# Gram of a DLRM tower: one 32x32 product per sample in two batches, and increments behind each gather instead of a memset

## What is computed

```python
e = jnp.stack([tbl_0[ids[:, 0]], ..., tbl_31[ids[:, 31]]], axis=1)      # 2048 x 32 x 64
gram = jnp.einsum('bnd,bmd->bnm', e, e)                                  # 2048 x 32 x 32
z = gram[:, rows, cols]                                                  # rows, cols = triu_indices(32, k=1)
h = jnp.concatenate([z.reshape(2048, -1), dense_ctx], axis=1)            # 2048 x 512
h = jnp.maximum(h @ W_top1 + b_top1, 0.0)                                # 512
h = jnp.maximum(h @ W_top2 + b_top2, 0.0)                                # 256
y = h @ W_top3                                                           # 1
```

## Time and profile before

| | us |
|---|---|
| median of 3 runs | 505.01 |
| lowest and highest | 502.04, 505.68 |
| the profiled execution | 506.08 |
| its span, from the first to the last instruction | 504.3 |
| busy: PE, POOL, DVE, ACT | 423.6, 417.8, 297.8, 114.6 |

### The profile page before, as it was taken

One profiled execution on the slowest core, in us unless ns is written; L12 is line 12 of the kernel. 1 busy time (PEld: TensorE's weight loads), 2 busy tenths in 40 slices (PEclk: granted clock), 3 DMA queues, 4 the chain that ended last, 5 costly groups with the idle time before them and its releaser, 6 DMA issues.

```text
span 504.3 us, 10183 instructions
## 1 busy us (share of the span) xinstructions
PE 423.6 (84%) x4080; PEld 382.6 (76%) x4080; DVE 297.8 (59%) x361; ACT 114.6 (23%) x206; POOL 417.8 (83%) x538
## 2 busy tenths in 40 slices
PE   5398589995299989979799969988999959993887
PEld 5387479984298879869698869868897949883765
DVE  2599779794094589448483749339753948250400
ACT  2244312131011321123012311132103300230311
POOL 7999999998898899888998989889998899885010
PEclk9699799997599999999799979999899979996999
DMA  4444631012301122112301123112311231111010
GB/s 109 140 141 149 205 137 22 17 33 51 102 15 23 25 60 98 22 26 61 102 17 24 40 57 88 22 27 56 102 21 21 54 84 44 24 35 44 1 43 2
DMA packets 22070, 29.58 MB, mean 59 GB/s; under 512 B 9910, under 2 KB 14198, under 8 KB 20896
## 3 DMA queue, kind: packets, MB, share of 16 engines
q1 hardware_dynamic: 12980, 18.96, 10.9%
q0 software_dynamic: 8640, 8.86, 10.7%
q10 hardware_dynamic: 404, 1.09, 0.5%
HBM read 24.61 MB, written 0.07 MB: 49 GB/s over the span
## 4 chain that ended last, share of the span: by engine, by line
POOL 82%; issue 9%; PE 4%; DMA 2%; SPq 1%; DVE 1%; ACT 1%; DVEq 0%; ACTq 0%
POOL rows L253 59%; POOL pause L260 23%; PE mlp_ps L328 1%; PE gram_ps L316 1%; SPq L192 1%; PE mlp_ps L338 1%; DVE folded L530 1%; ACT folded L441 0%; DMA rows<-tbl,index 0%; PE gram_ps L352 0%; SPq L219 0%; DMA index<-ids 0%; DMA pairs<-dense 0%; DMA pairs<-folded 0%; PE turn_ps L289 0%
## 5 line engine op out<-in xcount | busy, mean ns | idle before, releaser
L253 POOL DMA_INDIRECT rows<-tbl,index x264 | 299.4, 1134 | 45.9 <-issue 43.3
L303 PE MATMUL turn_ps<-split_sb,onehot 125*128 125x192 bf16 x2192 | 210.4, 256 | 19.9 <-DVE split_sb L544 17.3
L303 PEld LDWEIGHTS turn_ps<-split_sb,onehot 125*128 125x128 bf16 x2192 | 192.9, 102 | 27.8 <-DVE split_sb L544 18.7
L495 DVE TENSOR_TENSOR onehot<-place,codes_wide 125x2048 bf16<-125x2048 f16 (+1 forms) x127 | 168.1, 1325 | 7.3 <-DMA place<-ids_scratch 7.3
L260 POOL MEMSET pause<- 128x384 f32 x264 | 115.7, 438 | 0.2
L503 DVE TENSOR_REDUCE rows<-turn_ps 128x128 f32<-128x384 f32 x124 | 68.8, 556 | 70.8 <-PE turn_ps L303 68.1
L530 DVE COPY_PREDICATED folded<-second_sb,gram_ps 128x512 f32<-128x512 int32 x64 | 46.6, 729 | 81.8 <-ACT folded L441 81.7
L316 PE MATMUL gram_ps<-emb_t 64*128 64x128 f32 x1024 | 74.0, 286 | 3.3 <-DVE folded L530 3.3
L316 PEld LDWEIGHTS gram_ps<-emb_t 64*128 64x128 f32 x1024 | 62.7, 190 | 17.7 <-issue 13.3
L289 PE MATMUL mlp_ps<-ident_sb,rows 128*128 128x128 f32 x240 | 39.1, 288 | 40.8 <-DMA rows<-tbl,index 34.5
L441 ACT COPY folded<-gram_ps 128x512 f32<-128x512 f32 x64 | 37.5, 586 | 152.0 <-PE gram_ps L316 152.0
(11 more groups left out here) (28 smaller groups left out, 75.8 us busy)
## 6 DMA issues: line engine op xcount, KB each, us to landing
place<-ids_scratch SPq DMA_DIRECT2D x8, 1000.0 KB
rows<-tbl,index POOLq DMA_INDIRECT x264, 2.7
pairs<-folded SPq DMA_DIRECT2D x122, 32.0 KB
emb_t<-tbl SPq DMA_DIRECT2D x8, 250.0 KB
folded<-tbl SPq DMA_DIRECT2D x5, 312.5 KB
w_sb<-w SPq DMA_DIRECT2D x1, 1024.0 KB
place<-ids_scratch ACTq DMA_DIRECT2D x1, 750.0 KB
rows<-tbl SPq DMA_DIRECT2D x2, 312.5 KB
```

Of the source, the lines that this page charges most:

```text
L253: nc.gpsimd.indirect_dma_start(rows[:, s % 2, slot, t, :], None, tables[f][:, :], bass.IndirectOffsetOnAxis(index[:, s, t, f:f + 1], 0),). ...
L303: last = nc.tensor.matmul(turn_ps[:, u % 2].rearrange("p k b -> p (k b)")[:, t * PARTS * DIM:(t + 1) * PARTS * DIM], onehot[:, u % RING, c ...
L495: nc.vector.tensor_tensor(onehot[:, u % RING, 0:SPAN[u], :], place[:, parity, u, :].unsqueeze(1).to_broadcast([TP, SPAN[u], SUPER]), codes ...
```

## The change

The Gram product is made one sample at a time. `gram_batch` makes 256/2 = 128 products a batch and there are two batches a super tile. A product has the 32 columns of one sample as weights and as moving operand. It stands on the 64 partitions of its half t and writes the 32 partitions of `gram_ps` that belong to i (the sample's place in its quad). The products go i by i, with t innermost. The 32x32 result is all wanted, so a copy and a fold of 128x512 take 128 samples instead of 32: 2 of each a super tile instead of 8.

The step keeps its eight slots (`SLOTS`); the two Gram batches stand in slots 0 and 1 (`GRAM_IN_SLOT`), behind the lookups of these slots. `folded` gets a buffer for each parity and ACT's wait for the moves goes away. The moves start after slot 1. The semaphore `grams_begun` is incremented once a batch on PE.

On POOL the memset and its wait go away, and 12 increments of the semaphore `paused` stand behind each gather. The landing places of some small tables at the start change (`spare`).

```diff
+SLOTS = 8
+GRAM_BATCHES = 2
+GRAM_IN_SLOT = (0, 1)
+BATCH_Q = QUADS // GRAM_BATCHES
...
-PAUSE = 384
+PAUSE = 12
...
-        folded = sb("folded", [P, QUAD, HALF, QUADS], fp32)
+        folded = sb("folded", [P, 2, HALF, QUADS], fp32)
...
-        gram_ps = ps("gram_ps", [P, 2, TILES, BATCH_Q // TILES, 2, QUAD * HALF], fp32)
+        gram_ps = ps("gram_ps", [P, GRAM_BATCHES, TILES, BATCH_Q // TILES, FIELDS], fp32)
...
                         ).then_inc(rows_landed[s % 2][slot // GROUP_F], 16)
-                        before = next(pauses)
-                        if before:
-                            pool.wait_ge(paused, before)
-                        nc.gpsimd.memset(pause[:], 0.0).then_inc(paused, 1)
+                        for _ in range(PAUSE):
+                            pool.sem_inc(paused, 1)
...
             def gram_batch(s, k):
                 pe.wait_ge(second_copied, GRAM_EMPTY + GRAM_BATCHES * s + k - 1)
-                for u in range(BATCH_Q):
-                    quad = BATCH_Q * k + u
-                    t, q = u % TILES, (BATCH_Q * k + u) // TILES
-                    e = emb_t[DIM * t:DIM * (t + 1), QUAD * q:QUAD * (q + 1), :]
-                    last = nc.tensor.matmul(gram_ps[:, k % 2, t, u // TILES].rearrange("p h ij -> p (h ij)"),
-                                            e.rearrange("p b f -> p (b f)"),
-                                            e.rearrange("p b (h j) -> p h b j", h=2),
-                                            start=True, stop=True)
+                pe.sem_inc(grams_begun, 1)
+                for u in range(BATCH_Q // TILES):
+                    for i in range(QUAD):
+                        for t in range(TILES):
+                            e = emb_t[DIM * t:DIM * (t + 1), QUAD * (BATCH_Q // TILES * k + u) + i, :]
+                            last = nc.tensor.matmul(gram_ps[FIELDS * i:FIELDS * (i + 1), k, t, u, :], e, e,
+                                                    start=True, stop=True)
...
-                    gram_batch(s, k)
+                    if k in GRAM_IN_SLOT:
+                        gram_batch(s, GRAM_IN_SLOT.index(k))
...
+            def copy_first(s, k, parity):
+                act.wait_ge(gram_ready, GRAM_BATCHES * s + k + 1)
+                nc.scalar.copy(folded[:, parity, :, BATCH_Q * k:BATCH_Q * (k + 1)].rearrange("p j (q t) -> p j q t", t=TILES),
+                               gram_ps[:, k, :, :, 0:HALF].rearrange("p t q j -> p j q t")).then_inc(first_copied, 1)
...
-                    if k == 0 and (mlp or not ahead):
-                        act.wait_ge(pairs_moved, 16 * len(MOVES) * s)
-                    act.wait_ge(gram_ready, GRAM_BATCHES * s + k + 1)
-                    nc.scalar.copy(folded[:, :, :, BATCH_Q * k:BATCH_Q * (k + 1)].rearrange("p i j (q t) -> p (i j) q t", t=TILES),
-                                   gram_ps[:, k % 2, :, :, 0, :].rearrange("p t q ij -> p ij q t")).then_inc(first_copied, 1)
+                    if k in GRAM_IN_SLOT:
+                        copy_first(s, GRAM_IN_SLOT.index(k), parity)
...
+            def fold_second(s, k, parity):
+
+                dve.wait_ge(first_copied, GRAM_BATCHES * s + k + 1)
+                dve.sem_inc(folds_begun, 1)
+                nc.vector.copy_predicated(
+                    folded[:, parity, :, BATCH_Q * k:BATCH_Q * (k + 1)].rearrange("p j (q t) -> p j q t", t=TILES),
+                    second_sb[:].unsqueeze(2).unsqueeze(2).to_broadcast([P, HALF, BATCH_Q // TILES, TILES]),
+                    gram_ps[:, k, :, :, HALF:FIELDS].rearrange("p t q j -> p j q t")).then_inc(second_copied, 1)
```

More of the change, by code:

```diff
@@ L1 @@
 from contextlib import ExitStack
-from itertools import count
 import numpy as np
@@ L51 @@
 assert [u for units in TURN_UNITS + GRAM_UNITS for u in units] == list(range(UNITS))
-GRAM_UNITS += [[]] * (GRAM_BATCHES - len(GRAM_UNITS))
+GRAM_UNITS += [[]] * (SLOTS - len(GRAM_UNITS))
 READY_MADE = 3
-assert READY_MADE < RING and READY_MADE <= UNITS and not any(GRAM_UNITS[GRAM_BATCHES - READY_MADE + 1:])
+assert READY_MADE < RING and READY_MADE <= UNITS and not any(GRAM_UNITS[SLOTS - READY_MADE + 1:])
 SP_MOVES = 10
-PAUSE = 384
+PAUSE = 12
 MOVES = [(i, jq) for i in range(QUAD) for jq in range(QUAD)]
@@ L87, in slot_meaning @@
     assert sorted(rows.ravel()) == list(range(HIDDEN1))
-    return rows, np.tile(second, (QUAD, QUAD))
+    return rows, np.tile(second, (QUAD, 1))
 def build(nc, ids, tables, dense, w1, b1, w2, b2, w3, identity, second, looked_ids, codes, out):
@@ L114, in build @@
         y = sb("y", [1, BATCH], fp32)
-        pause = sb("pause", [P, PAUSE], fp32)
         w1_sb = sb("w1_sb", [P, CHUNKS, HIDDEN1], fp32)
@@ L121, in build @@
         ident_sb = sb("ident_sb", [P, P], fp32)
-        second_sb = sb("second_sb", [P, QUAD * HALF], i32)
+        second_sb = sb("second_sb", [P, HALF], i32)
         split_sb = sb("split_sb", [TP, SPAN_AT[-1], PARTS, DIM], bf16)
@@ L130, in build @@
         onehot = sb("onehot", [TP, RING, SPAN_MAX, SUPER], bf16)
-        spare = [(8, emb_t[0:TP].rearrange("p b f -> p (b f)")), (6, folded[0:TP].rearrange("p i j q -> p (i j q)")),
-                 (3, rows[0:TP, 1, 0:UNITS].rearrange("p u t d -> p (u t d)"))]
+        spare = [(8, emb_t[0:TP].rearrange("p b f -> p (b f)")), (1, h2[0:TP].rearrange("p o b -> p (o b)")),
+                 (3, folded[0:TP].rearrange("p h j q -> p (h j q)")),
+                 (3, rows[0:TP, 1, 0:UNITS].rearrange("p u t d -> p (u t d)")),
+                 (1, pairs[0:TP, 1].rearrange("p i j q -> p (i j q)"))]
         whole = []
@@ L185, in build @@
         folds_begun = sem("folds_begun")
+        grams_begun = sem("grams_begun")
         block = ctx.enter_context(nc.Block())
@@ L244, in _ @@
         def _(pool):
-            pauses = count()
             def gather(s, begin=UNITS):
@@ L366, in step @@
                     stay_warm(WARM_NEXT)
-                for k in range(GRAM_BATCHES):
+                for k in range(SLOTS):
                     if ahead:
@@ L520, in step @@
                         follow(s + 1, TURN_UNITS[g], 1 - parity)
-                for k in range(GRAM_BATCHES):
+                for k in range(SLOTS):
                     if ahead:
                         follow(s + 1, GRAM_UNITS[k], 1 - parity)
-                        if k >= GRAM_BATCHES - READY_MADE:
-                            make_onehot(s + 2, k - (GRAM_BATCHES - READY_MADE), parity, loads=loads)
+                        if k >= SLOTS - READY_MADE:
+                            make_onehot(s + 2, k - (SLOTS - READY_MADE), parity, loads=loads)
                     if mlp and k == LAYER3_BEFORE:
                         layer3_drain(s - 1)
-                    dve.wait_ge(first_copied, GRAM_BATCHES * s + k + 1)
-                    dve.sem_inc(folds_begun, 1)
-                    nc.vector.copy_predicated(
-                        folded[:, :, :, BATCH_Q * k:BATCH_Q * (k + 1)].rearrange("p i j (q t) -> p (i j) q t", t=TILES),
-                        second_sb[:].unsqueeze(2).unsqueeze(2).to_broadcast([P, QUAD * HALF, BATCH_Q // TILES, TILES]),
-                        gram_ps[:, k % 2, :, :, 1, :].rearrange("p t q ij -> p ij q t")).then_inc(second_copied, 1)
+                    if k in GRAM_IN_SLOT:
+                        fold_second(s, GRAM_IN_SLOT.index(k), parity)
             def take_high(u):
```

6 lines of the change are left out of this document (2 added, 4 removed).

## The result

The changed kernel is much slower: median 694.64 us (678.72 to 705.76, 4 runs) beside 505.35 (502.04 to 505.96, 4 runs), ratio 1.354, 95% interval 1.335 to 1.374. The forecast was 465 us, range 435 to 560. The profiled execution took 700.86 us. Medians and ranges are of all executions; the ratio compares only those that lie within 1.5% of the fastest of their kernel (here 678.72 and 688.42 us).

A forecast was written before the change was run, and what follows sets the result against it. POOL's gathers and memsets were taken to set the pace, with PE the bound once the memsets go: 372.8 + 8 x 11.3 = 463.2 us, with 1.8 around the span and the profiled run 1.1 above the median; predicted 465, range 435 to 560.

The forecast's parts named there:

- It becomes the bound when POOL gets faster: On PE: it has little slack, so its own need sets the time once POOL's 115.7 us of memsets go.
- 372.8 + 8G: Span in us as PE alone would set it: 372.8 without Gram, plus eight super tiles' Gram work.
- G: Gram work of one super tile on PE: 11.3 us taken, 8.7 to 34.8 as bounds.
- signs of being wrong: Gram batch over 8.2 us; 0.4 us gaps before gathers; granted clock falling in Gram batches, or PE standing at their start.
- Record time of a thin product: On PE: 22 ns for each of 512 Gram records a super tile, bounds 17 and 68 ns.
- increments under the gather: On POOL: increments of 0.07 us, 0.84 per gather, run while the gather runs; gather interval 1.3 us.
- increments behind the gather: Rival on POOL: increments run strictly after each gather, interval 2.13 us, POOL stays the bound, 576 us; chance 0.12.
- an unchanged interval: Rival on POOL: gathers come no closer without the memset, span stays near 504 us; chance 0.07.
- the likeliest case: Whole kernel: 17 to 26 ns a Gram record on PE, 444 to 481 us; chance 0.45.
- The pause at the loop's jump: On PE: a stand of 2.4 us, expected to be better covered by the long products of layer 2.
- the tail: From the end of the last Gram product to the end of the span: 28.0 us.
- the fixed price: Rival on PE: thin products do not shrink with their columns; 559 us at 45 ns, 653 at 68; chance 0.17.

The follow-up runs named there:

- e4: Kernel before with nothing behind the gathers, neither memset nor increments: 654.13 us.
- e7: Changed kernel, 12 increments, gathers fetching only 64 of 128 rows from super tile 2 on: 490.32 us.
- e8: Changed kernel without the gathers of super tiles 2 to 7 and their increments: 485.92 us.
- e9: Changed kernel, 12 increments, gathers fetching 128 bytes of each row instead of 256 from super tile 2 on: 484.61 us.
- e16: Changed kernel, 12 increments, gathers fetching 96 of 128 rows from super tile 2 on: 482.42 us.
- e13: Changed kernel with 14 increments behind each gather instead of 12: 486.8 us.
- e12: Kernel before without the gathers and memsets of super tiles 2 to 7: 474.44 us.
- e14: Kernel before with 14 increments behind each gather in place of the memset: 477.87 us.
- e2: Kernel before with 12 increments behind each gather in place of the memset and its wait: 555.96 us.
- e15: Kernel before with 13 increments behind each gather in place of the memset: 468.29 us, ratio 0.927.

## Why the prediction failed, step by step

**"It becomes the bound when POOL gets faster": the step that failed.** The working took PE's need (372.8 + 8G, 51.2 us a step) as independent of what POOL does, and the 115.7 us of memsets as time to be had. In the changed kernel the steps took 80 to 99 us, because while gathers ran PE got two or three products every 0.73 us. In the kernel before, the memset was not just a delay of POOL: with it gone and nothing else changed, the kernel goes from 504 to 654 us (e4, both on chip 8). No rival has PE lose its instructions, so no price and no chance stood for it. One of the signs of being wrong did come, a granted clock that falls in the Gram batches (0.50 from 217 to 238 us). That the memset's absence is not the whole condition, since the same gathers and increments ran without the trickle at the start of e7, e8, e9 and e16, is as far as the runs go; the cause behind it stays open.

**Record time of a thin product.** Forecast 22 ns, bounds 17 to 68. In a stretch undisturbed, e13 has 246 product records within 2.87 us, under 12 ns each on average, below my lower bound. The rule of the Trainium skill ("TensorE: Matmul & The Clock Gate", section "Wait — 56ns, not 53.3ns?") gave 25 ns as a floor; for these records, on alternating row halves, the trace disagrees, and the measurement decides. The timeline of e13:

```profile
238.27 2.87 PE L316 MATMUL gram_ps<-emb_t 64*32 64x32 f32 x246
242.75 0.27 PE L316 MATMUL gram_ps<-emb_t 64*32 64x32 f32 x10 [1.62 <-issue]
242.96 3.47 PE L302 MATMUL turn_ps<-split_sb,onehot 125*128 125x192 bf16 x40
246.36 2.51 PE L316 MATMUL gram_ps<-emb_t 64*32 64x32 f32 x204
250.30 0.65 PE L316 MATMUL gram_ps<-emb_t 64*32 64x32 f32 x52 [1.43 <-issue]
250.88 8.42 PE L302 MATMUL turn_ps<-split_sb,onehot 125*128 125x192 bf16 x100
```

The two batches take 4.69 and 4.52 us up to the next piece, G = 9.2 (forecast 11.3), and a third of it is a pause of 1.6 and 1.4 us in which PE has no instructions. So where G comes out near the forecast it is by luck: the record time was too high, and the pause was not in it. In the changed kernel as it is, the Gram of each of super tiles 1 to 5 took 32 to 39 us: the trickle takes whatever PE has to do while gathers run, lookups too, so no G describes it.

**The thin Gram is worth nothing on PE even then.** Before had 8.7 us a super tile, the thin one 9.2 to 11.8 in e13, pauses included, and after such a pause the next lookups can run at the low clock: in e8, 40 lookup products behind the pause of 2.45 us took 5.1 us at a granted clock of 0.66 instead of 3.4. These two are what the traces show of the 12 us between e12 and e8 (on two chips) and the 9 us between e14 and e13 (on one); their shares were not measured apart.

**POOL: increments under the gather.** Right in kind: 12 increments of 0.0785 us (I took 0.07) are 0.94 us, as long as a gather, and gathers stand 1.25 us apart where POOL catches up; 1.3 was forecast. "Or 12 increments and a start, about 1.0" was wrong: the loop itself needs 0.47 us beside them. The rivals of POOL, increments behind the gather and an unchanged interval, are both refuted.

**The sum for PE alone.** It was too low by itself, by about 30 us, which is more than the half-width of the likeliest case (444 to 481). For the thin Gram with its G of some 10 us it gives 372.8 + 80 + 1.8 = 455; the runs without the trickle have 482 to 490. For the Gram of before it gives 444, and e12 has 474. The steps are part of it: the first Gram product of two successive steps in e13 stands at 238.27 and 286.76, 48.5 us, but the four others between 128 and 395 us are 52 to 58 long, and the five together are 53.4 on average where 39.9 + 10 had been counted. The pause at the loop's jump, which was taken out as a wait, stays (in e13 two of 8.0 us together). Right were the tail (28.4 us from the last Gram product to the end in e13, forecast 28.0) and that the chain moves to PE, with no waits for rows.

**Chances.** "Slower" had 0.25, all of it with the fixed price or with POOL. The kernel ends on that side for neither reason, so that share was right by luck; 694.64 lies above even the bound of 68 ns a record (653).

## What to carry to other kernels

A pause that computes nothing may pay for something that no wait in the profile names: take it out alone before anything is built on its time. Short, regular idle times of an engine with nothing as their releaser mean that its instructions come late; look at what the other queues do in them. Count instructions as a resource: four times as many products with the same columns bought nothing (487 us against 478 with 14 increments, on one chip).

When a run differs from its reference, look first at the part that the edit leaves alone. If that part differs too, as the first two super tiles do here, the edit is not what made the difference. And put the reference itself, not only the kernel before, into every series: the kernel before had 504 to 507 us on each chip and showed nothing of what separates them.

## What the runs showed of the hardware

- While indirect gathers 0.94 us long run at 1.25 to 1.5 us distance, the issue of instructions on PE, and at times on POOL, can be held to one to three in 0.7 us (e4, e2, the changed kernel). The same gathers at the same distance can also run without it (e15, and the start of e8, with 12 increments).
- On one chip, what stood behind the gathers changed the time of the kernel with the Gram of before from 504 us (memset) over 556 (12 increments) to 654 (nothing).
- A semaphore increment on POOL takes 0.0785 us, a gather's issue about 0.47 beside them, and both run under the gather before.
- fp32 products of 64 rows and 32 columns on alternating halves start less than 12 ns apart on average (246 in 2.87 us, e13), and 512 instructions in a row run into a pause of 1.4 to 2.5 us.
